# Routed first layer of a graph-attention and mixture stack: odd tiles' weights copied by ScalarE, first chunk normalised alone, last products a pair sooner

## The reference, cut to what matters

```python
x = x + L0_gnn(layernorm(x), adj)      # 4-head graph attention over a 2048 x 2048 adjacency
x = x + L0_ffn(layernorm(x))           # mixture of 8 experts, two per row
x = x + L1_gnn(layernorm(x), adj)      # graph attention, one softmax for 4 heads
x = x + L1_ffn(layernorm(x))           # routed network, below

def L1_ffn(x):                         # route: an expert number for every 32 rows
    h = relu(x @ Wi.T + bi)            # 128 -> 256
    for l in range(2):
        shared = h @ Ws[l].T + bs[l]
        routed = h @ Wr[l, route].T + br[l, route]      # 16 experts, each 256 x 256
        h = relu(shared + routed + h)
    return h @ Wo.T + bo               # 256 -> 128
```

## Time and profile before

| | us |
|---|---|
| median of 3 runs | 693.85 |
| lowest and highest | 693.58, 696.41 |
| the profiled execution | 696.53 |
| its span in the trace | 694.8 |
| PE busy | 570.1 |
| DVE busy | 525.3 |
| ACT busy | 375.6 |
| Pool busy | 197.1 |

### The profile page before, as it was taken

One profiled execution on the slowest core, in us unless ns is written; L12 is line 12 of the kernel. 1 busy time (PEld: TensorE's weight loads), 2 busy tenths in 40 slices (PEclk: granted clock), 3 DMA queues, 4 the chain that ended last, 5 costly groups with the idle time before them and its releaser, 6 DMA issues.

```text
span 694.8 us, 13327 instructions
## 1 busy us (share of the span) xinstructions
PE 570.1 (82%) x5144; PEld 436.6 (63%) x5144; DVE 525.3 (76%) x882; ACT 375.6 (54%) x755; POOL 197.1 (28%) x222
## 2 busy tenths in 40 slices
PE   1835865999999999999989799999997554698965
PEld 1634754687776877877668475678795452366633
DVE  6699989875787667799678565979989999685430
ACT  1758888378776767776674655533413011243323
POOL 4200006021011100990422010022131022977731
PEclk9967897799999999999999898999999886899978
DMA  6454740010155055999797010021024252466530
GB/s 149 94 95 81 203 83 1 1 58 6 62 183 182 2 183 182 209 216 184 126 178 123 0 62 1 0 61 61 1 65 152 64 149 76 122 198 195 156 107 17
DMA packets 45219, 70.99 MB, mean 102 GB/s; under 512 B 4860, under 2 KB 24324, under 8 KB 45156
## 3 DMA queue, kind: packets, MB, share of 16 engines
q1 hardware_dynamic: 28804, 47.78, 21.9%
q0 software_dynamic: 15488, 22.02, 18.7%
q10 hardware_dynamic: 864, 0.33, 0.2%
HBM read 73.26 MB, written 22.02 MB: 137 GB/s over the span
## 4 chain that ended last, share of the span: by engine, by line
PE 59%; DVE 21%; ACT 10%; issue 5%; POOL 2%; POOLq 1%; DMA 1%; SPq 0%; ACTq 0%; DVEq 0%
PE bank L636 13%; PE bank L596 11%; PE bank L648 9%; DVE arena L1460 7%; PE bank L779 4%; PE bank L825 4%; ACT arena L1037 3%; PE bank L726 3%; PE bank L581 3%; PE bank L816 3%; DVE arena L1333 3%; DVE arena L1321 2%; ACT ysb L994 2%; PE bank L742 2%; PE bank L545 1%
## 5 line engine op out<-in xcount | busy, mean ns | idle before, releaser
L458 POOL TENSOR_TENSOR x<-x,ysb 128x512 f32<-128x512 f32 x36 | 70.8, 1967 | 261.5 <-ACT ysb L994 259.9
L1037 ACT ACTIVATE arena<-heads,nd 128x512 bf16<-128x512 f32 x192 | 122.2, 718 | 32.3 <-PE bank L596 32.3
L596 PE MATMUL bank<-reg_b,arena 128*128 128x99 bf16 x2048 | 102.1, 213 | 14.9 <-DVE arena L1333 14.7
L596 PEld LDWEIGHTS bank<-reg_b,arena 128*128 128x128 bf16 x2048 | 100.3, 101 | 17.8 <-issue 15.1
L636 PE MATMUL bank<-hTc,arena 128*128 128x512 f32 x192 | 95.9, 656 | 5.6 <-ACT reg_c L983 5.6
L1460 DVE SCALAR_TENSOR_TENSOR arena<-reg_b,nd,arena 128x1536 f32<-128x1536 f32 x48 | 91.2, 1962 | 0.0
L648 PEld LDWEIGHTS bank<-arena,reg_c 128*128 128x128 f32 x768 | 87.5, 192 | 4.8 <-issue 4.8
L1321 DVE TENSOR_TENSOR arena<-maskT,arena 128x2048 bf16<-128x2048 bf16 x48 | 61.4, 1279 | 36.9 <-ACT arena L1037 36.9
L1333 DVE TENSOR_TENSOR arena<-maskT,arena 128x2048 bf16<-128x2048 bf16 x64 | 87.0, 1359 | 2.2
L648 PE MATMUL bank<-arena,reg_c 128*128 128x128 f32 x768 | 87.8, 275 | 0.0
L983 ACT ACTIVATE reg_c<-bank,b 128x512 f32<-128x512 f32 x96 | 65.3, 687 | 27.0 <-PE bank L636 27.0
(11 more groups left out here) (176 smaller groups left out, 787.8 us busy)
## 6 DMA issues: line engine op xcount, KB each, us to landing
maskT<-routed_sums SPq DMA_DIRECT2D x48, 256.0 KB, 3.2
reg_c<-in_adj POOLq DMA_DIRECT2D x16, 512.0 KB, 6.1
arena<-in_w1T SPq DMA_DIRECT2D x16, 512.0 KB, 4.0
arena<-in_w2T SPq DMA_DIRECT2D x16, 512.0 KB, 5.1
routed_sums<-in_wsT SPq DMA_DIRECT2D x32, 256.0 KB, 5.4
routed_sums<-in_wrT POOLq DMA_DIRECT2D x32, 256.0 KB, 12.8
arena<-routed_sums SPq DMA_DIRECT2D x32, 256.0 KB, 3.0
routed_sums<-ident POOLq DMA_DIRECT2D x4, 1024.0 KB, 12.8
```

What stands on the lines that cost most here:

```text
L458: nc.gpsimd.tensor_tensor(xi, xi, ysb[:, e % 3, :].rearrange("p (t d) -> p t d", d=P), ALU.add).then_inc(s_acc, 1)
L596: last = mm(bank[i // 2][:, o:o + VW], ind[:, q, b, j, i * P:(i + 1) * P], u[:, (t * H + h) * 2 + b, :, :], start=(t == 0 and i % 2 == 0 a ...
L1037: last = af(ind[:, q, 1, j, :], sbc[:, h, :], ACT.Relu, bias=nd[:, q * QT + j, h:h + 1], scale=BIG)
```

## The change

Four things change, all around the routed network.

- `w_first` and `prob` change places: the weights' slots now lie in `reg_c`, the probability tiles in the arena's first 4096 columns.
- The first pair's weights (tiles 0 and 1) come by eight DMAs of SP straight from `routed_sums`, ahead of the 16 loads of `kept`. Pool's `select` now copies the even tiles 2 to 14 alone. ACT has a `select` of its own for the odd tiles 3 to 15: two copies behind the evictions of `turn` in each layer.
- DVE merges and normalises chunk 0 alone, then makes tiles 2 and 3, then merges chunks 1 and 2 and does their statistics, then scales chunk 1.
- PE's products for the fourth chunk stand in other places of `expert_pair`, which has a third place for them, between the last `turn` and `output`; tile 15 is multiplied in the fifth pair, not the sixth. ACT takes the sums in that pair.

```diff
-        w_first = arena[:, 0:4096].rearrange("p (s k n) -> p s k n", s=2 * GT, k=KC)
...
-        prob = reg_c[:, :].rearrange("p (s i) -> p s i", s=8)
+        w_first = reg_c[:, :].rearrange("p (s k n) -> p s k n", s=2 * GT, k=KC)
+        prob = arena[:, 0:4096].rearrange("p (s i) -> p s i", s=8)
...
             sp.wait_ge(s_skip, 16 * L * KC)
+            for n in range(2 * GT):
+                e = sp.value_load(route[0:1, n:n + 1], min_val=0, max_val=E1 - 1)
+                sp.dma_start(w_first[:, n, :, :].unsqueeze(1),
+                             routed[:, 0, bass.ds(e, 1), :].rearrange("p o (k n) -> p o k n", k=KC)
+                             ).then_inc(s_pair, 16)
...
-                    pe.wait_ge(s_copy, t + 1)
+                if l == 0 and t < 2:
+                    pe.wait_ge(s_pair, 16 * 2 * GT)
+                elif l == 0:
+                    pe.wait_ge(s_odd if t % 2 else s_even, t // 2)
...
+                for t in products[L]:
+                    attend1(t)
...
+            def select(t, groups):
+
+                for g in groups:
+                    e = act.value_load(route[0:1, t * GT + g:t * GT + g + 1], min_val=0, max_val=E1 - 1)
+                    last = af(w_first[:, GT + g, :, :].rearrange("p k n -> p (k n)").unsqueeze(1),
+                              kept[:, bass.ds(e, 1), :], ACT.Copy)
+                if g == GT - 1:
+                    last.then_inc(s_odd, 1)
...
+                        if t < T:
+                            select(t, range(l * GT // L, (l + 1) * GT // L))
...
+            dve.wait_ge(s_v1, C)
             last_tiles(0, 2)
```

More of the change, by code:

```diff
@@ L225, in gnn_moe_stack @@
         s_kept = sem("first_routed_layer_loaded")
-        s_copy = sem("first_routed_layer_selected")
+        s_pair = sem("first_pair_of_routed_tiles_loaded")
+        s_even = sem("even_tile_weights_selected")
+        s_odd = sem("odd_tile_weights_selected")
         s_second = [sem(f"second_routed_layer_slot{r}_loaded") for r in range(4)]
@@ L487, in select @@
             def select(t):
-                if t >= 2:
-                    pool.wait_ge(full[3 + t % 2 * 2], (BANK5 if t % 2 else BANK3) + (t - 2) // 2 * (L + 1) + 1)
+                pool.wait_ge(full[3], BANK3 + (t - 2) // 2 * (L + 1) + 1)
                 for g in range(GT):
                     e = pool.value_load(route[0:1, t * GT + g:t * GT + g + 1], min_val=0, max_val=E1 - 1)
[L493 to L496, removed]
+                    last = nc.gpsimd.tensor_copy(w_first[:, g, :, :].rearrange("p k n -> p (k n)").unsqueeze(1),
+                                                 kept[:, bass.ds(e, 1), :])
+                last.then_inc(s_even, 1)
             one_hot(0)
@@ L500, in _ @@
             pool.wait_ge(s_kept, 16 * E1)
[L501 to L504, removed]
             for c in range(C):
@@ L512, in _ @@
                 for i in range(CT):
[L513 to L516, removed]
+                    if i % 2 == 0 and c * CT + i + 2 < T:
+                        select(c * CT + i + 2)
                     pool.wait_ge(ev["y"], FFN_Y + c * CT + i + 1)
@@ L889, in _ @@
             ln_transpose(6, odiv)
[L890 to L895, removed]
+            expert_pair(0, 0, ((), (), ()))
+            expert_pair(0, 2, ((2,), (3,), ()), xn)
+            expert_pair(1, 0, ((), (4,), ()))
+            expert_pair(1, 2, ((5, 6, 7), (8,), ()), odiv)
+            expert_pair(2, 0, ((9, 10), (11, 12, 13), (14, 15)))
+            expert_pair(2, 2, ((), (), ()))
             ln_transpose(6, xn)
-            expert_pair(3, 0, ((), ()))
-            expert_pair(3, 2, ((), ()))
+            expert_pair(3, 0, ((), (), ()))
+            expert_pair(3, 2, ((), (), ()))
         @block.scalar
@@ L1203, in _ @@
                             ln_out()
-                        if i == 2 and l == 1 and c == C - 2:
-                            sums(3 * (P + 1), P + 1)
                         for j in (i, i + 1):
                             turn(j, l)
+                        if t < T:
+                            select(t, range(l * GT // L, (l + 1) * GT // L))
+                        if i == 0 and l == 1 and c == C - 2:
+                            sums(3 * (P + 1), P + 1)
                     for j in (i, i + 1):
@@ L1511, in _ @@
             divisors(WT, reg_b)
-            merge1(0, WT, 0, reg_b).then_inc(s_attf, 1)
+            then(merge1(0, CT, 0, reg_b))
+            norm(0, 2 * C + 4, odiv)
+            last_tiles(2, 2)
+            merge1(CT, 2 * CT, CT, reg_b).then_inc(s_attf, 1)
             dve.wait_ge(s_attf, C * H + 1)
-            norms(3, 2 * C + 4)
-            last_tiles(2, 2)
+            for c in range(2):
+                last = statistics((c + 1) * CT, c * CT)
+            then(last)
+            deviations(2 * CT)
+            scale(CT, xn)
             last_tiles(4, QT)
             dve.wait_ge(ev["hTc"], 2 * C + 5)
-            scale(2 * CT, odiv, 2 * CT)
+            scale(2 * CT, odiv, CT)
             last_tiles(8, QT)
```

3 lines of the change are left out of this document (2 added, 1 removed).

## The result

| | before | after |
|---|---|---|
| median, us | 695.13 (4 runs) | 674.05 (4 runs) |
| lowest and highest | 693.58, 696.66 | 669.86, 674.41 |
| the profiled execution | 696.53 | 673.83 |
| its span | 694.8 | 672.0 |

The ratio is 0.9686, with a 95% interval of 0.9655 to 0.9718: 21 us less, where 16.9 us were forecast.

A forecast was written before the change was run, and what follows sets the result against it. PE was taken to bound the kernel, with 24.9 us of long waits after 567 us. Gains of 23.4 us, less 6 for ACT and 0.5 for Pool, gave 16.9 us: 693.85 to 677.0 us, range 671.5 to 685.0.

The forecast's parts named there:

- Step 1: First chunk merged and normalised alone: PE's first transposition 6.6 us sooner, the first pair staying slow.
- Step 2: Weights for tiles 2 to 15: PE's 6.07 and 1.23 us waits for Pool and the slow clock go, 8.6 us.
- rival (a): Pool shut out by DVE in the new order, delaying copies for tiles 4 and 6: 681 us, chance 0.15.
- SP's loads: First pair's eight loads ahead of those of `kept` in SP's queue: 8.48 us, costed at nothing.
- Step 3: End of the fourth chunk's attention: PE's 5.39 us wait and the slow clock behind it go, 8.2 us.
- rival (b): Tiles 12 to 15 late, PE waits 3 us in the fifth pair: about 683 us, chance 0.10.
- Step 4: ACT's 28 copies on the path between pairs: six times 1.0 us, 6 us lost.
- Half a microsecond for Pool: Allowance in the sum for remaining waits on Pool: half a microsecond lost.
- (c): ACT's 28 copies wholly on the path, 18.8 us against 23.4 gained: 689.3 us, chance 0.10.
- (d): ACT's sequencer does not run ahead over register loads, 1.7 us a copy: slower, 702 us, chance 0.04.
- (e): ACT's copy of tile 3 too late, so the wait at 601.62 only changes its releaser: 680 us, chance 0.05.

The follow-up runs named there:

- u1: Changed kernel with chunks 0 to 2 merged and normalised together again, as before the change; 682.95 us, ratio 0.984.
- u4: Changed kernel with the weights of tiles 0 and 1 copied by Pool once the sums are complete, not loaded by SP; 675.96 us, ratio 0.973.
- b1: Kernel before with DVE's new order alone: Pool makes all copies, no loads by SP, products in their old places; 687.16 us, ratio 0.9888.
- v2: Changed kernel plus seven filler products on PE that nobody reads, in its idle time ahead of the first transposition; 675.46 us, ratio 0.9732.
- u2: Changed kernel with Pool copying the odd tiles 3 to 15 as well and no copies on ACT; 678.59 us, ratio 0.9749.
- u3: Changed kernel with the fourth chunk's products back in their old places; 680.9 us, ratio 0.98.
- a1: Changed kernel without ACT's 28 copies and PE's wait for them, so odd tiles 3 to 15 use tile 1's first-layer weights; 672.77 us, ratio 0.9703.
- u5: u1 with one wait more: DVE starts tiles 4 to 7 only when Pool has copied tile 2's weights; 682.56 us, ratio 0.9862.
- v1: Changed kernel with Pool, not ACT, copying tiles 13 and 15; 670.2 us, ratio 0.9655.
- a2: Changed kernel with each of ACT's 28 copies made twice, the first time into unused columns; 684.58 us, ratio 0.9848.

## Why the prediction was right, point by point

The forecast was 16.9 us; from the reciprocal to the last product the traces show 118.79 - 96.77 = 22.0 us.

**Step 1**, 6.6 us forecast: 13.46 - 6.62 = 6.84 us measured. The two causes that I had named both show: u1 puts 3.80 us on the eight further merges and bn_stats, u4 puts 2.62 us on Pool's copies. b1, with the new order and Pool's copies, splits it the same way: 13.46 - 9.26 = 4.20 us for the order, 9.26 - 6.62 = 2.64 us for the copies. The first pair stayed slow as I said (10.96 against 10.87 us), and v2 shows that the idle time is why. One time in this step was added up wrong: tiles 4 to 7 at the slow pace would end at 588.7 + 17.5 = 606.2, not at 604. They ended at 601.0, ahead of PE's first use of them at 605.5.

**Step 2**, 8.6 us forecast: in pair 2 it was 18.41 - 11.38 = 7.03 us, with 0.44 us of ACT's copies in it, and in pair 4 the 1.23 us wait went. The number is right and the cause is not, so that the number came out is luck. I gave both waits to the split between Pool and ACT. b1 has no split and neither wait; u1 has the split and the 6 us wait. The 6.07 us were rival (a)'s mechanism, Pool shut out by DVE, at work in the kernel before, and I had the row for it and put it among the rivals as something that might come. What I said of the timing in step 2 (DVE at merges and bn_stats, copies done near 585) is in effect the true reason: Pool's four copies ran from 581.26 to 584.47. The split has its worth elsewhere, in DVE's tiles (u2). SP's loads, which I had put at nothing, did cost nothing: the issues of `kept` end at 551.1 us, before at 551.8.

**Step 3**, 8.2 us forecast: u3 gives 8.90 us. DVE was in time with the tiles. It made tiles 12 to 15 from 617.83 to 628.5 at 0.67 us an operation, so the nearness that I feared (tile 12 between 629 and 634) was not there, and rival (b) did not come.

**Step 4**, 6 us forecast, is the mis-sized term: 2.5 us measured (a1). I had the gap behind the first `turn` right, and the copies at 0.64 us. The step that failed is the slide of the next `hidden` evictions, which I put at 0.9 us for each of six pairs. It is 0.5 us at three places and 0.26 to 0.29 at the three behind attention products, which I had not told apart. From the end of the second `turn` to `hidden` I had 689.7 - 687.61 = 2.09 us; the trace has 657.15 - 655.41 = 1.74. The copies took 1.43 us until the first `output`, not 1.59, and the two `output` evictions, both queued by then and started 0.16 us apart, 0.31 us, not 0.5.

**The rest.** Half a microsecond for Pool was not needed. The fifth pair got the products of three more tiles and grew by 14.76 - 12.32 = 2.44 us, 0.8 us a tile, where the products of two tiles take 2.05 us: those between `turn` and `output` fill a wait for ACT. So 3.5 + 0.5 + 0.6 us for these and 0.2 us from step 1 make most of the difference of 5 us.

**The rivals.** (a), a shut-out in the new order, did happen, but where nobody waits: an addition of Pool stood 6.5 us while DVE made tiles 12 to 15.

```profile
617.83 2.73 DVE L1476 SCALAR_TENSOR_TENSOR arena<-hT,nd,maskT 128x512 f32<-128x512 f32 x4
620.48 5.38 DVE L1476 SCALAR_TENSOR_TENSOR arena<-hT,nd,arena 128x512 f32<-128x512 f32 x8
```
```profile
622.30 6.94 POOL L518 TENSOR_TENSOR x<-x,ysb 128x128 f32<-128x128 f32 x2 [6.26 <-ACT ysb L1195]
```

In a1, an even smaller edit, it hit tile 4's weights and PE waited 3.03 us, where I had priced tile 4 at 0.5 us. In the changed kernel the same copy began at 590.58 us, 1.7 us after DVE's row of tiles began, alternated with DVE, and its four copies took 3.91 us; in a1 it began 1.05 us after. Why one gets in and the other doesn't stays open, so that the changed kernel escapes is partly luck. (c) and (d), ACT's copies wholly exposed or serial with their loads, are excluded by a1 and by the copies' 0.64 us from one to the next. (e) did not come.

## What to carry to other kernels

Where an idle engine waits for a Pool operation that is far longer than its fellows, look at what DVE runs beside it before taking work from Pool: a gap in DVE's row may do more than half the copies (b1), though it can also just move the stall (u5). Before moving Pool's work in time, look at what DVE has to finish then: in u2, u4, v1 and v2 Pool's copies slowed DVE, and PE paid for it. Extra work on an engine that stands between two others costs what is left after its gaps, so place it against the timeline, and expect the next portion to cost more than the first: here 9.2 us against 2.5, and its full length where no gap is left. And measure from a common event inside the trace when the parts ahead of it wander by several microseconds.

## What the runs showed of the hardware

- **Pool can be shut out by DVE for far longer than one operation.** Operations of DVE and Pool that read SBUF either alternate (1.01 us from one to the next of DVE's instead of 0.67, Pool's copies 1.0 instead of 0.65) or Pool stands until DVE's row ends: 11.28 us in before, 11.04 in u1, 10.10 in a1, 9.92 in a2, 9.53 in u5, 6.5 in after, with DVE not slowed at all. The Trainium skill, page SBUF — State Buffer, section "SBUF: two separate sides", has the second one blocked for the whole instruction of the first; the traces show it blocked for up to sixteen instructions more. What decides between the two I could not settle: Pool's start within DVE's operation does not sort the cases (both occur at 0.35 us behind its start, and at 0.5), nor does a long rest of Pool (after 1.7 us it got in, after 2.14 us in a1 it did not, after 3.74 us in u5 it did). One side does hold in all fourteen traces: every operation of Pool that was shut out for over 3 us had rested 2.14 us or more, and none that had rested less was. Whether the rest is the cause, no run tests.
- **Tiny DVE operations pay too.** With Pool's copies beside them, operations of 4 elements per partition went from 0.17 to as much as 0.58 us (u4), while bn_stats stayed at 0.87 us for four. The scale's four operations, 1.11 us alone, took 2.30 us in v2.
- **The clock.** Behind 5.4 us of idle time PE ran at its lower level (granted clock 0.50 from 574 to 578 us), with filler products in the same place at the upper one (1.00, v2), which ties the slow phase to the idle time. Shorter waits fell out both ways: behind 2.93 us in u2 eight products took 2.09 instead of 1.16 us (granted 0.50), behind 3.03 us in a1 sixteen took the full-speed 1.09 (granted 1.00).
